# A recurrent four-layer kernel: the second layer's feed-forward jobs every third scan unit, and its layer norm among the last scan units

## The reference, cut to what matters

```python
# L1 attention: B 4, L 256, D 256, E 512 features, N 16 states
def step(h, inp):
    x_t, d_t, b_t, c_t = inp
    h = jnp.exp(d_t[:, :, None] * A) * h + (d_t * x_t)[:, :, None] * b_t[:, None, :]
    y = jnp.einsum('ben,bn->be', h, c_t)
    return (h, y)
y = y + x * W_D
y = y * jax.nn.silu(skip)
return resid + y @ W_out.T

# L1 feed-forward: INTER 1024
h = jnp.square(jax.nn.relu(jnp.einsum('bsh,hi->bsi', residuals, up_w)))
y = jnp.einsum('bsi,ih->bsh', h, down_w) + moe_out
mu = y.mean(axis=-1, keepdims=True)
var = jnp.mean(jnp.square(y - mu), axis=-1, keepdims=True)
return (y - mu) * jax.lax.rsqrt(var + EPS) * ln_gamma + ln_beta
```

## Time and profile before

| | us |
|---|---|
| median of 3 runs | 1128.98 |
| the runs | 1126.83, 1128.98, 1131.62 |
| the profiled execution's own time | 1134.37 |
| its span in the profile | 1132.6 |
| TensorE, matmul busy | 1010.6 (89%) |
| VectorE busy | 756.2 (67%) |
| ScalarE busy | 498.8 (44%) |
| GpSimd busy | 379.1 (33%) |

### The profile page before, as it was taken

How to read it: one execution, slowest core, us unless ns; L and a number is a source line. 1 busy time by engine, 2 the same in 40 slices (tenths; PEclk the granted TensorE clock), 3 DMA queues, 4 the chain that set the end, 5 groups by cost and what they waited for, 6 DMA issues and landing times. The chain is left out here.

```text
span 1132.6 us, 14814 instructions
## 1 busy us (share of the span) xinstructions
PE 1010.6 (89%) x4900; PEld 666.6 (59%) x4900; DVE 756.2 (67%) x1218; ACT 498.8 (44%) x1135; POOL 379.1 (33%) x284
## 2 busy tenths in 40 slices
PE   5799867965999999859979989996899989999997
PEld 4355554624566566545558868884566658555554
DVE  3689965325999999757628868827566640765762
ACT  3542324266888788334124434423566641111112
POOL 0379910005888788510011221210355540000000
PEclk9899988885999999878889999997999999999999
DMA  4112104003000000022022332381000000101001
GB/s 118 39 60 85 50 16 156 1 7 107 19 25 24 19 26 4 1 59 65 1 87 61 87 86 67 83 233 57 1 2 2 1 1 12 45 30 53 28 0 38
DMA packets 53917, 52.55 MB, mean 46 GB/s; under 512 B 10088, under 2 KB 48840, under 8 KB 53856
## 3 DMA queue, kind: packets, MB, share of 16 engines
q1 hardware_dynamic: 50256, 47.05, 13.8%
q0 software_dynamic: 3072, 4.20, 2.2%
q10 hardware_dynamic: 528, 0.52, 0.1%
HBM read 44.19 MB, written 5.47 MB: 44 GB/s over the span
## 5 line engine op out<-in xcount | busy, mean ns | idle before, releaser
L1017 POOL TENSOR_TENSOR seen<-state,c_row 128x512 f32<-128x512 f32 x128 | 160.5, 1275 | 39.9 <-PE banks L1155 27.7
L1037 DVE TENSOR_TENSOR_SCAN state<-decay,banks 128x512 f32<-128x512 f32 x128 | 155.5, 1217 | 21.0 <-issue 7.3
L2300 PE MATMUL banks<-xnT,weight 128*128 128x512 f32 x256 | 115.0, 593 | 1.0 <-PEq L2027 1.0
L976 ACT ACTIVATE weighed_x<-dx_tok,b_tok 128x512 f32<-128x512 f32 x128 | 90.1, 709 | 25.3 <-PE banks L1141 25.0
L2034 POOL TENSOR_TENSOR prob<-prob,inverse 128x512 f32<-128x512 f32 x64 | 65.2, 1039 | 107.5 <-DVE inverse L2119 107.5
L1141 PEld LDWEIGHTS banks<-ident,weighed_x 128*128 128x128 f32 x512 | 59.5, 142 | 63.9 <-ACT weighed_x L976 40.5
L986 ACT ACTIVATE decay<-delta_pairs,A 128x510 f32<-128x510 f32 x128 | 90.5, 707 | 6.3 <-DVE state L1037 6.2
L1141 PE MATMUL banks<-ident,weighed_x 128*128 128x128 f32 x512 | 81.0, 282 | 6.9 <-ACT weighed_x L976 6.0
L2341 DVE TENSOR_TENSOR inter<-gelu,banks 128x512 f32<-128x512 f32 x32 | 22.0, 688 | 96.7 <-ACT gelu L2332 96.1
L2332 ACT ACTIVATE gelu<-banks 128x512 f32<-128x512 f32 x32 | 19.1, 597 | 138.2 <-PE banks L2300 138.2
L2300 PEld LDWEIGHTS banks<-xnT,weight 128*128 128x128 f32 x256 | 48.7, 190 | 49.2 <-issue 47.7
(11 more groups left out here) (363 smaller groups left out, 2046.8 us busy)
## 6 DMA issues: line engine op xcount, KB each, us to landing
prob_row<-probs_dram SPq DMA_DIRECT2D x8, 512.0 KB, 4.2
c_row<-c_dram SPq DMA_DIRECT2D x32, 128.0 KB, 2.9
slot_gate_w<-in_L_ffn_w_gate SPq DMA_DIRECT2D x16, 176.0 KB
slot_up_w<-in_L_ffn_w_up SPq DMA_DIRECT2D x16, 176.0 KB
slot_down_w<-in_L_ffn_w_down SPq DMA_DIRECT2D x16, 176.0 KB
gate_up_w<-in_L_ffn_gate_up_w SPq DMA_DIRECT2D x8, 256.0 KB, 4.3
delta_pairs<-conv_in SPq DMA_DIRECT2D x8, 256.0 KB, 3.4
w_WqT<-in_L_attn_W_q SPq DMA_DIRECT2D x1, 2048.0 KB, 10.0
```

The lines of the kernel that those rows point to most:

```text
L976: nc.scalar.activation(weighed[:, v % 2, tile, :, j, :], dx_tok[:, 4 * p + tile, :].rearrange("p (g e) -> p g e", g=groups), ACT.Identity, ...
L1017: nc.gpsimd.tensor_tensor(seen[:, u % ring, :], state[:, u % ring, :], c_row[:, v % 4, :], ALU.mult).then_inc(seen_ready, 1)
L1037: nc.vector.tensor_tensor_scan(state[:, u % ring, :], decay[:, u % ring, :, :].rearrange("p b t -> p (b t)"), banks[:, 4 + u % 2, :], 0.0, ...
L2300: last = nc.tensor.matmul(banks[:, 4 + 2 * half + j, :], weight[:, s, j, k, tile * P:(tile + 1) * P], xnT[:, k, cols[half]], start=(k == 0 ...
```

## The change

Three things change in `scan_stage`:
- Jobs take three units each (`pitch = 3`), so they end at unit 95. In job v, `raise_` and `rectify` stand both in unit 3v, `square` in 3v + 1 and `lower` in 3v + 2. `add_lowered(b)` stands at units 26, 50, 74 and 98, the two `bn_stats` of sequence b three units later (`spread`).
- The layer norm of `y` moves into the last units: `variance` at unit 108, Sqrt on ScalarE at 116, reciprocal and offset (`shift`) at 118, one Identity in each of units 120 to 127, `gamma(0)` to `gamma(2)` at 121, 123 and 125, `gamma(3)` behind the loop. The waits for the late weights move with them. Beta and Silu stay behind the loop.
- Behind the loop VectorE has `gamma(3)`, the four gates, and `mix(b)`, `finish(b)` in turn for each b. `lower(31)` is no more behind TensorE's loop.

The diff:

```diff
--- before.py
+++ after.py
@@ -902,6 +902,8 @@
     ring = 4
     jobs = BATCH * INTER1 // P
     tiles = INTER1 // P
+    pitch = 3
+    normed = units - groups
     with ExitStack() as ctx:
         m = Core(nc, ctx)
         c_row = m.sbuf("c_row", [P, 4, HALF])
@@ -994,13 +996,15 @@
                     decays(u)
                     if u + groups < units:
                         weigh(u + groups)
-
-                act.wait_ge(var_ready, 1)
-                nc.scalar.activation(std[:, :], var[:, :], ACT.Sqrt).then_inc(std_ready, 1)
-                act.wait_ge(offset_ready, 1)
-                for t in range(NT):
-                    nc.scalar.activation(y[:, t, :], y[:, t, :], ACT.Identity, bias=offset[:, t:t + 1],
-                                         scale=rstd[:, t:t + 1]).then_inc(norm_ready, 1)
+                    if u == normed - 4:
+                        act.wait_ge(var_ready, 1)
+                        nc.scalar.activation(std[:, :], var[:, :], ACT.Sqrt).then_inc(std_ready, 1)
+                    if u >= normed:
+                        t = u - normed
+                        act.wait_ge(offset_ready, 1)
+                        nc.scalar.activation(y[:, t, :], y[:, t, :], ACT.Identity, bias=offset[:, t:t + 1],
+                                             scale=rstd[:, t:t + 1]).then_inc(norm_ready, 1)
+
                 for b in range(NT // 2):
                     act.wait_ge(beta_ready, b + 1)
                     nc.scalar.activation(y[:, 2 * b:2 * b + 2, :], y[:, 2 * b:2 * b + 2, :], ACT.Silu
@@ -1017,15 +1021,19 @@
                     nc.gpsimd.tensor_tensor(seen[:, u % ring, :], state[:, u % ring, :], c_row[:, v % 4, :], ALU.mult
                                             ).then_inc(seen_ready, 1)
 
-                for u in range(units):
-                    see(u)
-                pool.wait_ge(*late_weights)
-                for b in range(NT // 2):
+                def beta(b):
                     two = slice(2 * b, 2 * b + 2)
                     pool.wait_ge(gamma_ready, b + 1)
                     nc.gpsimd.tensor_tensor(y[:, two, :], y[:, two, :],
                                             w["ln_beta"][:, :].unsqueeze(1).broadcast_to([P, 2, D]), ALU.add
                                             ).then_inc(beta_ready, 1)
+
+                for u in range(units):
+                    see(u)
+                    if u == units - 8:
+                        pool.wait_ge(*late_weights)
+                for b in range(NT // 2):
+                    beta(b)
 
             @block.vector
             def _(dve):
@@ -1062,6 +1070,33 @@
                     nc.vector.tensor_tensor(y[:, two, :], y[:, two, :], banks[:, 7, :].rearrange("p (t d) -> p t d", t=2),
                                             ALU.add).then_inc(y_ready, 1)
 
+                steps = Steps(dve, y_steps)
+
+                def spread(b):
+                    dve.wait_ge(y_ready, b + 1)
+                    for t in range(2 * b, 2 * b + 2):
+                        steps.add(nc.vector.bn_stats(stats[:, t, :], y[:, t, :]))
+
+                def variance():
+                    steps.join()
+                    for t in range(NT):
+                        steps.add(nc.vector.bn_aggr(mean_var[:, t, :], stats[:, t, :]))
+                    steps.join()
+                    nc.vector.tensor_scalar(var[:, :], mean_var[:, :, 1], EPS, None, ALU.add).then_inc(var_ready, 1)
+
+                def shift():
+                    dve.wait_ge(std_ready, 1)
+                    steps.do(nc.vector.reciprocal(rstd[:, :], std[:, :]))
+                    nc.vector.scalar_tensor_tensor(offset[:, :], mean_var[:, :, 0], -1.0, rstd[:, :], ALU.mult, ALU.mult
+                                                   ).then_inc(offset_ready, 1)
+
+                def gamma(b):
+                    two = slice(2 * b, 2 * b + 2)
+                    dve.wait_ge(norm_ready, 2 * b + 2)
+                    nc.vector.tensor_tensor(y[:, two, :], y[:, two, :],
+                                            w["ln_gamma"][:, :].unsqueeze(1).broadcast_to([P, 2, D]), ALU.mult
+                                            ).then_inc(gamma_ready, 1)
+
                 for q in range(ring):
                     nc.vector.memset(decay[:, q, :, 0:1], 0.0).then_inc(cleared, 1)
                 dve.wait_ge(cleared, ring)
@@ -1069,42 +1104,28 @@
                 for u in range(units):
                     if u + 1 < units:
                         scan(u + 1)
-                    if u % 4 == 2:
-                        rectify(u // 4)
-                    if u % 4 == 3:
-                        square(u // 4)
+                    if u < pitch * jobs and u % pitch == 0:
+                        rectify(u // pitch)
+                    if u < pitch * jobs and u % pitch == 1:
+                        square(u // pitch)
                     if u == pass_units + 2:
                         for mi in range(MI):
                             gate(0, mi)
-                    b, r = divmod(u - 5, 4 * tiles)
-                    if r == 0 and b:
+                    b, r = divmod(u - 2, pitch * tiles)
+                    if r == 0 and 0 < b <= BATCH:
                         add_lowered(b - 1)
-                add_lowered(BATCH - 1)
+                    if r == 3 and 0 < b <= BATCH:
+                        spread(b - 1)
+                    if u == normed - 12:
+                        dve.wait_ge(*late_weights)
+                        variance()
+                    if u == normed - 2:
+                        shift()
+                    if u > normed and (u - normed) % 2 == 1 and u < units - 1:
+                        gamma((u - normed) // 2)
+                gamma(BATCH - 1)
                 for mi in range(MI):
                     gate(1, mi)
-
-                steps = Steps(dve, y_steps)
-                dve.wait_ge(y_ready, BATCH)
-                for t in range(NT):
-                    steps.add(nc.vector.bn_stats(stats[:, t, :], y[:, t, :]))
-                steps.join()
-                for t in range(NT):
-                    steps.add(nc.vector.bn_aggr(mean_var[:, t, :], stats[:, t, :]))
-                steps.join()
-                nc.vector.tensor_scalar(var[:, :], mean_var[:, :, 1], EPS, None, ALU.add).then_inc(var_ready, 1)
-                dve.wait_ge(std_ready, 1)
-                steps.do(nc.vector.reciprocal(rstd[:, :], std[:, :]))
-                nc.vector.scalar_tensor_tensor(offset[:, :], mean_var[:, :, 0], -1.0, rstd[:, :], ALU.mult, ALU.mult
-                                               ).then_inc(offset_ready, 1)
-
-                dve.wait_ge(*late_weights)
-
-                def gamma(b):
-                    two = slice(2 * b, 2 * b + 2)
-                    dve.wait_ge(norm_ready, 2 * b + 2)
-                    nc.vector.tensor_tensor(y[:, two, :], y[:, two, :],
-                                            w["ln_gamma"][:, :].unsqueeze(1).broadcast_to([P, 2, D]), ALU.mult
-                                            ).then_inc(gamma_ready, 1)
 
                 def mix(b):
 
@@ -1117,18 +1138,9 @@
                     dve.wait_ge(s_ready, b + 1)
                     add_gated(nc, dve, b, x_tok, s_tok[:, 2 * b:2 * b + 2, :], y, gate_ready, x_ready, x_stats)
 
-                gamma(0)
-                mix(0)
-                gamma(1)
-                mix(1)
-                gamma(2)
-                gamma(3)
-                mix(2)
-                finish(0)
-                finish(1)
-                mix(3)
-                finish(2)
-                finish(3)
+                for b in range(NT // 2):
+                    mix(b)
+                    finish(b)
 
             @block.tensor
             def _(pe):
@@ -1187,16 +1199,15 @@
                     if u == pass_units + 3:
                         for mi in range(MI):
                             begin(1, mi)
-                    if u % 4 == 0:
-                        raise_(u // 4)
-                    if u % 4 == 2 and u > 4:
-                        lower(u // 4 - 1)
+                    if u < pitch * jobs and u % pitch == 0:
+                        raise_(u // pitch)
+                    if u < pitch * jobs and u % pitch == 2:
+                        lower(u // pitch)
                     if u % 2 and u > 2:
                         total(u - 3)
                         total(u - 2)
                 total(units - 2)
                 total(units - 1)
-                lower(jobs - 1)
                 pe.wait_ge(gated_ready, passes * MI)
                 for t in range(NT):
                     for k in range(MI):
```

## The result

| | before | after |
|---|---|---|
| median, us | 1129.01 (4 runs, 1126.83 to 1131.62) | 1150.28 (4 runs, 1149.67 to 1158.40) |
| ratio to before, 95% interval | | 1.0186 (1.0151 to 1.0220) |
| the profiled execution, span | 1134.37, 1132.6 | 1149.67, 1147.9 |
| last see ends (E), counted from the first drive | 194.33 | 225.30 |
| last finish, counted from E | 28.75 | 18.95 |

The change costs 21 us. Forecast were 13.7 us and 1142.7, with a range up to 1150.0; the direction was right, the size too small, and the median lies 0.3 us above the range, which is less than the spread of the runs. The rows from E on are read from the timelines. "Counted from the first drive" takes out what happens ahead of the loop: +30.97 up to E, -9.80 in the tail, +21.17 in all, as much as the medians say.

What follows compares the result with a forecast made beforehand. The prediction took the loop before to be TensorE-bound and the tail a chain. It summed +23.8 us up to E and -10.1 in the tail to +13.7 on the median of 1128.98: 1142.7 us, range 1132 to 1150.

Steps and rivals of the forecast that it cites:

- What bounds the loop before: Scan loop of the kernel before: TensorE is full, 1.445 us a unit, with no room for a denser stretch.
- (a): Jobs every third unit: TensorE's load is 9.53 us per six units, 1.59 a unit if nothing waits.
- (b): New wait of rectify for raise_: 10.36 us per six units, VectorE waiting about 0.6 and 1.6 us a round.
- R1: Rival: the relu wait is hidden and the loop runs at TensorE's 1.59 a unit; 1129.5 us, 10%.
- (e): Last 30 units: VectorE and GpSimd tie; with loads, Identity wait and gammas, E is 492.5, +23.8 us.
- (c): Four gates and begins at unit 66 stand on the chain: 2.8 us, between 2.5 and 4.
- (d): Where the job stretch ends: drive(2) at 280.79, last round starts at 439.0, see(97) ends at 452.1.
- R3: Rival: ScalarE's two table loads are dearer, by a drain of 1.38 us each; 1145.3 us, 7%.
- (f): Tail behind the last see: W_out at about E + 1.9, clock stays, end at E + 18.6; gain 10.1 us.
- R2: Rival: TensorE's clock falls in small pauses of the last third or around E, costing 3.3 us; 1146 us, 18%.
- R4: Rival: the last third is bound elsewhere, moved work meeting the scans badly; about +5 us, 1148, 8%.

Runs made afterwards that it cites:

- relu_later: The changed kernel with rectify and square one unit later and lower with the job after: 1134.08 us, ratio to before 1.0022.
- add_in_idle: The changed kernel with add_lowered moved from behind scan(24b+3) to ahead of rectify at unit 24b: 1144.15 us, one run.
- norm_behind: The changed kernel with the whole layer norm behind the loop, in the order of before: 1153.64 us, ratio to before 1.0184.
- four_gates_first: The kernel before with the four gates of the second pass ahead of add_lowered(3): 1125.32 us, ratio to before 0.9950.
- no_root: The changed kernel with an Identity in place of the Sqrt at unit 116, so both table loads are gone: 1146.50 us, one run.
- sqrt_twice: The changed kernel with a second Sqrt at unit 112, into a tile that nothing reads: 1153.02 us, one run.
- four_short_tail: The kernel before with gates first, bn_stats of three sequences in the loop, mix and finish in turn: 1125.38 us, ratio to before 0.9936.

## Why the prediction was wrong, point by point

- **What bounds the loop before**, and (a) TensorE's 1.59 a unit: right; relu_later shows 9.56 for six units where 9.53 was worked out.
- **(b) the relu wait**: right to 0.01 us a round, and right in mechanism: VectorE's two waits are 1.59 and 0.57 for 1.6 and 0.6, and relu_later takes them out. That the sum of so many links came out to 0.01 is also luck, since each was read to no better than that. R1, that it is hidden, falls.
- **The step that failed is the one that was not written.** The prediction priced `add_lowered` as 0.6 us of VectorE time, once, in (e). It stands in `lower` that the first of a sequence waits for `y_ready`; before, the add came at unit 32b + 5, behind scan(32b + 6), and that `lower` at 32b + 6, behind a drive that waits for the same scan. The change puts both into unit 24b + 2: the add now stands behind scan(24b + 3), while the drive ahead of `lower` waits for scan(24b + 2) only, so TensorE comes a scan too early. The prediction worked out what waits for the relu, but not what waits for the add, and so had this wait at nothing. Three times 1.49 us, 4.5 in all; add_in_idle shows it.
- **(c) the gates**: 3.9 and not 2.8, inside the stated 2.5 to 4. The reason given, that TensorE issues most begins while the gates run, did not hold: 1.96 of their 3.70 us lie behind the last gate. The begins are eight matmuls 0.43 us apart, 3.4 us of TensorE; in the kernel before and in relu_later, where TensorE is full, the round with the gates is longer by just that (12.13 for 8.69, 12.99 for 9.56, from drive to drive). So 2.8 was too low from the rows of before.
- **(d)**: the first relu came 0.5 us later behind the first drive than worked out. The last six matmuls of the begins ahead of drive(2) ran longer than before:

```profile
275.79 3.76 PE L1160 MATMUL banks<-xs,diag_D 128*128 128x512 f32 x6
```

They took 3.16 in the kernel before, where the granted clock went from 1.2 to 2.4 GHz 4.31 us behind the first drive; here it was 5.52. That is a difference of two profiled executions and not of the change: in the kernels of the experiments, with the same code there, it is 4.20 to 5.48.
- **(e) the last 30 units**: from the last even relu to E the prediction had 51.9 and it took 52.9 (444.71 to 497.62). The tie of VectorE and GpSimd is right: without the norm GpSimd needs 1.234 a unit, and the 30 units take 37.20 us (norm_behind) for the 36.9 forecast. With the norm they take 41.35, so it costs 4.15 where 3.5 stood. The loads were put at 0.9 and cost 0.5. The gammas were put at 1.8 above their own time of 1.8; taking them out gives 1.9, and GpSimd bounds as soon as they are gone. The remaining 1.75, for the statistics, the offset and the wait of Identity(0), stood at 0.8. Small operations are held too, which was not counted: `y_offset`, 128x8, took 0.67 us in place of 0.17. The three gammas of the loop, 1.03, 0.92 and 1.17 us long, each end 0.54 or 0.55 behind the end of the see that was running when they began, and `y_offset` ends 0.03 behind it; the fourth gamma took 0.66, and see(127), which started in it, 1.58 in place of 1.27. The Trainium skill, "SBUF — State Buffer", section "Who interferes with whom", says that a VectorE operation with two SBUF inputs contends with a GpSimd one that reads SBUF, and that the shared port pair is an exclusive lock. These rows agree with it.
- **R3** falls: in the loops of all these timelines a load takes 1.28 us, starts 0.02 behind the activation ahead of it, and the activation that waits for it starts 0.01 behind its end. The Trainium skill, "ScalarE: Activation LUTs", section "What ACT_TABLE_LOAD costs", gives about 1283 ns for the load and about 1380 ns more for a drain. The load agrees; the drain is in none of these timelines.
- **(f) the tail**: -10.1 forecast, -9.80 measured; W_out at E + 1.90 for 1.9, end at E + 18.95 for 18.6, clock kept, so R2 falls, and R4 with it: the last units came out 1.0 us over the forecast where R4 had 5. The reason given for the tail named lower(31), the add and the norm together. The runs part them: four_gates_first shows 4.1 us for the gates and W_out being early and at the full clock, norm_behind 5.3 for that and the last `lower` and add being gone, and the last 4.5 come with the norm's new place and the order of `mix` and `finish`; the loop took them back. (For R2 the prediction put the fall of the clock 3 us into a pause; it fell at 473.19, 2.35 us into it.)

The sum: 4.5 (adds) + 1.1 (gates) + 0.5 (start) + 1.0 (last units) + 0.3 (tail) = 7.4 of the 7.5 us by which the stage missed the forecast. On the range: it was set around the terms that stood in the sum; for a term that was overlooked it had nothing on the slow side.

## What to carry to other kernels

Before work is packed denser beside a loop, find what the loop is bound by. Where an engine is full, as TensorE here, denser jobs in one part cost their load there (13.9 us), and the part without them gives back only as much as the next engine allows (3.9 us). Then list each wait of the moved steps, the rare ones (once in eight jobs) too, and check on both engines how many units the consumer stands behind its producer: the two edges that the change put into one unit cost 0.8 us a round and 1.49 us a time, and a unit or two of distance took them away. And read the tail by itself: one operation that waits for something late, standing ahead of the work that feeds the long last part, was worth 4.1 us here, more than all of the rearrangement.

## What the runs showed of the hardware

- Table loads and activations of ScalarE stand back to back, 0.01 to 0.02 us apart. A pair of loads with its root, 2.8 us long, cost the loop 0.5 us where ScalarE had a lead of 2.31 us (no_root); a second pair four units ahead of it cost 4.9 us more (sqrt_twice), about half of it the loads and the rest a fall of TensorE's clock.
- VectorE operations with two SBUF operands stretch beside GpSimd's: gammas 0.66 to 1.17 us, a 128x8 operation 0.17 to 0.67, the product in `finish` 0.69 to 1.72. GpSimd's stretch as well: the see that started within a gamma took 1.58 us in place of 1.27, the betas of four_short_tail 1.67.
- TensorE's granted clock was 1.00 (2.4 GHz) in the changed kernel from 277.8 to 516.8 us of its span. It stayed there through two pauses of 0.29 and 0.14 us in each undisturbed round, three of 1.39 ahead of `lower`, pauses of 0.35 to 0.96 in the last 30 units, and the 0.78 ahead of W_out. In the kernel before it fell to 0.50 (1.2 GHz) at 473.19, 2.35 us into the pause of 3.17 us ahead of W_out, and was back at 480.02, with TensorE busy since 474.01; the first quarter of W_out took 6.7 us there, the others 3.44. In sqrt_twice it fell in the same way at 481.54, 2.12 us into a pause of 3.17, and was back at 488.37.
